# q and k of the first attention in three fp32r passes from operands that GpSimd splits

## The chip, the cores and the metric

One core of one Trainium2 chip. The time is device microseconds of one execution of the whole program. The engines are TensorE (PE; PEld is its weight load), VectorE (DVE), ScalarE (ACT), GpSimd (POOL) and SyncE (SP, which issues the DMAs).

## What is computed

Two transformer layers on x of shape (8, 512, 128), each an attention and a feed-forward part with a residual and a layernorm behind each. The change touches the projections of the first attention only:

```
qkv = x @ W_qkv                                  # (8, 512, 128) @ (128, 384), fp32
q, k, v = jnp.split(qkv, 3, axis=-1)             # 16 heads of 8
scores = einsum('bhnd,bhmd->bhnm', q, k) / sqrt(128)
out = einsum('bhnm,bhmd->bhnd', softmax(scores), v)
x = layernorm(x + out)
```

The kernel takes q and k on as exact sums of three bf16 parts, so the projections have to come out in nearly full fp32 precision.

## The kernel before

Each engine runs one program of its own, and semaphores tie them together. `attention0` (from L304) is a software pipeline over the eight batches, walked by `walk` (L282) in the same way on every engine: a step has 32 units u, and a unit takes two of the 64 turns of S1. It starts with a lead step of batch -1, which has no softmax work, and a loop of three rounds holds two steps each. While step b does S2 (`s2`, L636: scores with the row maximum folded in), the exponentials on ACT (L497) and the product with v (`pv`, L650) of batch b, it also does S1 of the batch ahead (`s1`, L572: scores for the row maximum alone, one 128x512 tile a turn) and brings in the batch after that. DVE takes the maximum of each S1 tile straight from PSUM (`reduce_max`, L735, L741), one instruction a turn.

S1 tiles and guests share three PSUM banks in turn (`FB`, `TURNS`, `BANK`). A guest stands in the list ahead of the turn that `GUEST_AT` gives: v at 16, q at 25, k at 33. `free_bank` (L582) makes PE wait until the turn that had the same bank before, three places back in the list, is taken out of it. After every two units four products with v stand between two S1 tiles on PE.

`qk_product` (L566) is one fp32 matmul of 128x512: `w[:, n, :]` is the stationary operand and `xt`, the batch's x with the model dimension on the partitions, the moving one. It waits for the load of `xt` alone. ACT copies the result to `qk` (`take_qk`, L476), and POOL splits that into three bf16 parts (`split_qk`, L819, by `split_in_parts`, L270), which SP writes to DRAM and reads back stacked by heads. Batch 0 is projected in another way ahead of the pipeline (L698).

POOL takes its work strictly in the order of its program. In a step this is (`units`, L829): the split of the row maxima (`split_max`), the residual add and layernorm of the batch behind (`add_x`, `layernorm_pool`, `layernorm_apply_pool`, L166 to L176), then `split_qk` of q and of k for batch b + 2, then the other half of the row maxima. The layernorm follows DVE's statistics, which stand in DVE's program at turn 16 (`STATS_AT`). SP loads `xt` of batch b + 2 at the start of its step b (`load_xt`, L382). Ahead of the loop, SP's `load_more` (L480) waits until all weights of the later stages are in. The same fp32r split of an x on POOL exists already at the end of this stage (`Front.gpsimd`, L957 and L960), and `hidden_lo` and the expert products use fp32r operands in three passes (L1979 to L1981).

Of the kernel before, what the change touches and what calls it, by code (L numbers as in the profile page):

```python
# [303 lines left out]
def attention0(outer, nc, g, x_t, w_qkv, select, load_more, more_in, e, m, wide):  # L304
# [4 lines left out]
    with ExitStack() as ctx:  # L309
# [3 lines left out]
        def sem(name):  # L313
            return outer.enter_context(nc.semaphore("a0_" + name))
# [15 lines left out]
        sel = prob[:, PSLOTS - 1, :, :].rearrange("p i t -> p (i t)").bitcast(BF16)[:, 0:2 * PARTS * PLACED * (HALF + QKR)]  # L330
        sel = sel.rearrange("p (n a j m) -> p n a j m", n=2, a=PARTS, j=PLACED)
        pool_gate = sb("pool_gate", [P, 1])
        nmax = sb("nmax", [P, 2, 2, HH * NT // 2])
        mrest = sb("mrest", [P, 2, HH * NT // 2])
        msplit = sb("msplit", [P, 2, PARTS, HH * NT // 2], BF16)
# [6 lines left out]

        w_in, x_in, xt_in = sem("w_in"), g["x_in"], [sem(f"xt_in{i}") for i in range(2)]
        cleared = sem("cleared")
        q_done, k_done, v_done = sem("q_done"), sem("k_done"), sem("v_done")
        q_taken, k_taken, v_taken = sem("q_taken"), sem("k_taken"), sem("v_taken")
        split, parts_done = sem("split"), sem("parts_done")
# [191 lines left out]
        def _(pe):  # L539
# [25 lines left out]

            def qk_product(b, p, n):  # L566

                pe.wait_ge(xt_in[p], 8 * (b - p) + 16)
                nc.tensor.matmul(ps_f[:, BANK["qk"[n]], :], w[:, n, :], xt[p][:, :], start=True,
                                 stop=True).then_inc((q_done, k_done)[n], 1)  # L570

            def s1(b, p, n, bank):  # L572

# [217 lines left out]
        @block.gpsimd  # L791
        def _(pool):
            pool.sem_inc(parts_done, 2 + PARTS_C)
            pool.sem_inc(parts_out, 2 * OUT_C)
            pool.sem_inc(split, 6)
            pool.sem_inc(mt_parts, MP_C)

            def split_max(b, half_no):

                k = 2 * b + half_no  # L800
                src = nmax[:, half_no, :, :]
                zero = g["zero"][:, :].unsqueeze(2).broadcast_to(list(mrest.shape))
                pool.wait_ge(mt_done, k)
                pool.wait_ge(max_done, S1_N * b + S1_N // 2 * (half_no + 1))
                nc.gpsimd.tensor_tensor(msplit[:, :, 0, :], src, zero, ALU.add).then_inc(mt_chain, 1)  # L805
                pool.wait_ge(mt_chain, 3 * k + 1)
                nc.gpsimd.tensor_tensor(mrest[:, :, :], src, msplit[:, :, 0, :], ALU.subtract).then_inc(mt_chain, 1)
                pool.wait_ge(mt_chain, 3 * k + 2)
                nc.gpsimd.tensor_tensor(msplit[:, :, 1, :], mrest[:, :, :], zero, ALU.add).then_inc(mt_chain, 1)
                pool.wait_ge(mt_chain, 3 * k + 3)  # L810
                nc.gpsimd.tensor_tensor(msplit[:, :, 2, :], mrest[:, :, :], msplit[:, :, 1, :],
                                        ALU.subtract).then_inc(mt_parts, 1)

            def add_x(b):

                pool.wait_ge(att_done, NO * (b + 1) + ATT_C)
                nc.gpsimd.tensor_tensor(att[:, :, :], att[:, :, :], X[:, b, :, :], ALU.add).then_inc(sum_done, 1)

            def split_qk(b, n):  # L819

                if isinstance(b, int) and b == 1:
                    pool.wait_ge(first_out[0], OUT_C // 2)
                    pool.wait_ge(first_out[1], OUT_C // 2)
                pool.wait_ge(parts_out, OUT_C * b + OUT_C)
                pool.wait_ge((q_taken, k_taken)[n], b + 1)
                split_in_parts(pool, nc.gpsimd, qk[:, n, :], rest[:, n, :], parts[:, n, :, :], 2 * b + n, split,
                               parts_done, g["zero"][:, :].broadcast_to([P, T]))

            def units(b, p, u0, u1, qk_on, fore, back, tail):  # L829
                if u0 == 0 and back:  # L830
                    split_max(b, 1)
                if u0 == 0 and is_first(b):
                    front.split_weight(pool, 0)
                if u0 == 0 and tail:
                    add_x(b - 1)
                    layernorm_pool(nc, pool, g, ln, b - 1)
                    layernorm_apply_pool(nc, pool, g, ln, b - 1, att, pool_gate)
                if u1 == NU and qk_on:
                    split_qk(b + 2, 0)
                    split_qk(b + 2, 1)  # L840
                if u1 == NU and fore:
                    if isinstance(b, int) and b == NB - 2:
                        pool.wait_ge(ln["x_done"], NB - 1)
                        front.split_weight(pool, 1)
                        front.split_weight(pool, 2)
                    split_max(b + 1, 0)
                    if isinstance(b, int) and b == NB - 2:
                        front.split_weight(pool, 3)
                        front.split_weight(pool, 4)
                        front.split_weight(pool, 5)  # L850
                if u1 == NU and is_last(b):
                    front.gpsimd(pool)

            pool.wait_ge(x_in, 16)
            walk(pool, units)

# [1721 lines left out]
```

## Time and profile before

| | |
|---|---|
| median of 3 runs (lowest to highest) | 1043.27 us (1043.18 to 1043.75) |
| span of the profiled execution | 1041.4 us |
| own time of the profiled execution | not listed apart from its span; the median stands 1.87 us above the span |
| busy: PE, DVE, ACT, POOL | 96%, 80%, 70%, 46% of the span |
| first attention | about 0 to 400 us of the span |
| one step of its loop | 44.15 us |

The busy share of an engine is its share of the span over all four stages. PE's busy time is modelled and counts the drain of each matmul, so two matmuls that follow each other overlap in it. What a turn costs is read from the starts of instructions instead, and from the idle time in front of them, which the timeline gives in brackets with the engine that ended it. A matmul of fp32 operands is recorded as two matmuls (x2), one of fp32r or bf16 operands as one.

### The profile page before, as it was taken

The numbers are of one execution on the slowest core, as the hardware profiler recorded it, in microseconds if no ns is written. First come the engines' busy times: TensorE is split into PE (matmuls) and PEld (weight loads), VectorE is DVE, ScalarE is ACT, GpSimd is POOL, SyncE is SP. The second block draws the span as 40 slices with busy tenths as digits, with TensorE's granted clock in tenths as the row PEclk, the third lists the DMA queues.
The fourth block names the chain that finished last, engine by engine and source line by source line (L and its number), as shares of the span: only waits on it lengthen the run. The fifth ranks groups of instructions, "written<-read, shape, count | busy, mean of one in ns | idle before, by whom it ended". The sixth has DMA issues, their size and how long they took to land. (4 is left out here: it accounts for less than half of the span.)

```text
span 1041.4 us, 20120 instructions
## 1 busy us (share of the span) xinstructions
PE 995.5 (96%) x5835; PEld 475.4 (46%) x5835; DVE 834.0 (80%) x1874; ACT 729.9 (70%) x939; POOL 475.6 (46%) x483
## 2 busy tenths in 40 slices
PE   8899999999999999999999999999999999999996
PEld 3222222222222235888888887873332333222485
DVE  6889999999999977787888789897666666643677
ACT  2078777787777786555555555568898888899754
POOL 0332514325053725676777677576442244220275
PEclk9999999999999999999999999999999999999998
DMA  6553222131321003344324323443512331230011
GB/s 198 153 186 119 76 76 89 44 117 46 96 78 52 3 2 101 102 128 145 101 91 156 121 90 117 137 137 102 172 65 61 121 119 63 60 122 1 1 31 52
DMA packets 73981, 97.04 MB, mean 93 GB/s; under 512 B 12669, under 2 KB 42237, under 8 KB 73533
## 3 DMA queue, kind: packets, MB, share of 16 engines
q1 hardware_dynamic: 73928, 96.40, 29.7%
q8 instruction: 26, 0.43, 0.2%
q14 instruction: 27, 0.21, 0.1%
HBM read 68.18 MB, written 27.79 MB: 92 GB/s over the span
## 5 line engine op out<-in xcount | busy, mean ns | idle before, releaser
L741 DVE TENSOR_REDUCE a_nmax<-a_ps_f 128x1 f32<-128x512 f32 x512 | 320.1, 683 | 20.2 <-PE a_ps_f L579 19.7
L497 ACT ACTIVATE a_prob<-a_ps_s 128x1024 f32<-128x1024 f32 x256 | 251.7, 1023 | 77.8 <-PE a_ps_s L646 76.5
L1367 ACT ACTIVATE a_prob<-a_ps_s 128x1024 f32<-128x1024 f32 x256 | 244.4, 1026 | 28.0 <-PE a_ps_s L1419 26.7
L2187 POOL TENSOR_TENSOR moe_hl<-moe_hid,moe_hh 128x512 fp32r<-128x512 f32 x134 | 173.9, 1303 | 84.3 <-ACT moe_hh L2068 84.2
L579 PE MATMUL a_ps_f<-a_ks,a_qs 48*128 48x512 bf16 x512 | 157.9, 386 | 11.8 <-DVE a_nmax L741 4.3
L2058 ACT ACTIVATE moe_ps<-moe_ps 128x512 f32<-128x512 f32 x128 | 74.5, 582 | 111.5 <-PE moe_ps L1981 110.7
L1432 PE MATMUL a_ps_o<-a_prob,a_va 128*32 128x512 f32 x1024 | 136.4, 605 | 1.4 <-DVE a_turned_o L1547 0.5
L659 PE MATMUL a_ps_o<-a_prob,a_va 128*32 128x512 f32 x1024 | 136.4, 605 | 0.5 <-ACT a_prob L497 0.4
L646 PE MATMUL a_ps_s<-a_qs,a_ks 51*128 51x512 bf16 x512 | 132.5, 381 | 1.7 <-ACT a_prob L497 1.5
L579 PEld LDWEIGHTS a_ps_f<-a_ks,a_qs 48*128 48x128 bf16 x512 | 39.7, 93 | 192.2 <-DVE a_nmax L741 162.2
L2109 DVE TENSOR_TENSOR moe_prod<-moe_cw,moe_ps 128x512 f32<-128x512 f32 x128 | 87.2, 681 | 27.4 <-PE moe_ps L1981 26.7
L1419 PE MATMUL a_ps_s<-a_qs,a_ks 48*128 48x512 bf16 x512 | 91.1, 384 | 12.0 <-ACT a_prob L1367 10.3
L2118 DVE TENSOR_TENSOR moe_hid<-moe_prod,moe_ps 128x512 f32<-128x512 f32 x128 | 86.9, 679 | 6.1 <-DVE moe_prod L2109 1.9
L2068 ACT ACTIVATE moe_hh<-moe_hid 128x512 fp32r<-128x512 f32 x136 | 84.9, 624 | 6.0 <-DVE moe_hid L2118 5.8
L277 POOL TENSOR_TENSOR a_parts<-a_qk,g_zero 128x512 bf16<-128x512 f32 x28 | 29.2, 1044 | 118.6 <-DVE a_qk L1529 60.8
L1419 PEld LDWEIGHTS a_ps_s<-a_qs,a_ks 48*128 48x128 bf16 x512 | 23.1, 93 | 130.0 <-ACT a_prob L1367 105.4
L805 POOL TENSOR_TENSOR a_msplit<-a_nmax,g_zero 128x32 bf16<-128x32 f32 x16 | 3.8, 238 | 144.9 <-DVE a_nmax L741 144.9
L1979 PE MATMUL moe_ps<-moe_xh,moe_whig 128*128 (+1 forms) x136 | 55.0, 405 | 1.3 <-DVE moe_hid L2118 1.3
L2006 PE MATMUL moe_ps<-moe_hl,moe_whid 128*128 128x512 f32 x136 | 53.9, 397 | 1.0 <-POOL moe_hl L2187 1.0
L1979 PE MATMUL moe_ps<-moe_xh,moe_whiu 128*128 (+1 forms) x136 | 53.7, 395 | 0.0
L2001 PE MATMUL moe_ps<-moe_hh,moe_wlod 128*128 128x512 f32 x136 | 53.7, 395 | 0.0
L1980 PE MATMUL moe_ps<-moe_xh,moe_wlog 128*128 (+1 forms) x136 | 53.7, 395 | 0.0
(302 smaller groups left out, 1640.1 us busy)
## 6 DMA issues: line engine op xcount, KB each, us to landing
moe_cw<-r_weights SPq DMA_DIRECT2D x256, 128.0 KB, 2.9
parts_q<-a_parts SPq DMA_DIRECT2D x48, 256.0 KB, 2.5
parts_k<-a_parts SPq DMA_DIRECT2D x48, 256.0 KB, 2.5
a_qs<-parts_q SPq DMA_DIRECT2D x126, 96.0 KB, 2.4
a_ks<-parts_k SPq DMA_DIRECT2D x126, 96.0 KB, 2.5
a_xt<-in_x_t SPq DMA_DIRECT2D x8, 256.0 KB, 2.8
out_x<-g_X SPq DMA_DIRECT2D x7, 256.0 KB, 2.3
moe_wg<-in_wg SPq DMA_DIRECT2D x1, 1088.0 KB, 6.6
```

The source lines that it names most:

```text
L497: nc.scalar.activation(prob[:, u % PSLOTS, :, :], ps_s[:, u % 2, :, :], ACT.Exp, scale=float(P) ** -0.5).then_inc(exp_done, 1)
L579: nc.tensor.matmul(ps_f[:, bank, :], stack_rows(qs[p], h, QKR)[:, qt * P:(qt + 1) * P], stack_rows(ks[p], h, QKR), start=True, stop=True). ...
L646: mm = nc.tensor.matmul(ps_s[:, u % 2, i, :], stack_rows(ks[p], h, MXR)[:, kt * P:(kt + 1) * P], stack_rows(qs[p], h, MXR), start=True, st ...
L659: mm = nc.tensor.matmul(ps_o[j * CT:(j + 1) * CT, :], v_of_head(va[p], kt, grp * HG + j), prob[:, (2 * e + j // UN) % PSLOTS, j % UN, :], ...
L741: nc.vector.tensor_reduce(nmax[:, half_no, h % 2, col:col + 1], ps_f[:, bank, :], AX.X, ALU.max, negate=True).then_inc(max_done, 1)
L1367: nc.scalar.activation(prob[:, u % PSLOTS, :, :], ps_s[:, u % 2, :, :], ACT.Sigmoid, scale=float(HD) ** -0.5).then_inc(exp_done, 1)
L1419: mm = nc.tensor.matmul(ps_s[:, u % 2, i, :], stack_rows(ks[p], h, QKR)[:, kt * P:(kt + 1) * P], stack_rows(qs[p], h, QKR), start=True, st ...
L1432: mm = nc.tensor.matmul(ps_o[j * CT:(j + 1) * CT, :], v_of_head(va[p], kt, grp * HG + j), prob[:, (2 * e + j // UN) % PSLOTS, j % UN, :], ...
L1979: nc.tensor.matmul(dst, w[0][:, j, :], hi, start=True, stop=False)
L2109: nc.vector.tensor_tensor(prod[:, bank(j), :], cw[:, slot(j), :], ps_u[:, bank(j), :], ALU.mult).then_inc(prod_done, 1)
L2118: nc.vector.tensor_tensor(hid[:, hid_at(j), :], prod[:, bank(j), :], ps_g[:, bank(j), :], ALU.mult).then_inc(hid_done, 1)
L2187: nc.gpsimd.tensor_tensor(hl[:, part_at(j), :], hid[:, hid_at(j), :], hh[:, part_at(j), :], ALU.subtract).then_inc(hl_done, 1)
```

## The change

q and k of batches 1 to 7 are computed from split operands. POOL splits the q and k columns of the weights once at the start (`part_w`: wh is w rounded to fp32r, wl the rest), and each batch's x ahead of its products (`part_x`: xh and xl, one buffer each). PE computes wh.xh + wl.xh + wh.xl in three matmuls into the same bank and waits for `x_parted`, which POOL raises, where it waited for the load. In a step, `part_x` stands in POOL's program between the layernorm of the batch behind and `split_qk`. Batch 0 and v are as before.

```diff
+        wh, wl = (sb(name, [P, 2, P], F32R) for name in ("wh", "wl"))
+        xh, xl = (sb(name, [P, T], F32R) for name in ("xh", "xl"))
...
             def qk_product(b, p, n):

-                pe.wait_ge(xt_in[p], 8 * (b - p) + 16)
-                nc.tensor.matmul(ps_f[:, BANK["qk"[n]], :], w[:, n, :], xt[p][:, :], start=True,
-                                 stop=True).then_inc((q_done, k_done)[n], 1)
+                dst = ps_f[:, BANK["qk"[n]], :]
+                pe.wait_ge(x_parted, 2 * b)
+                nc.tensor.matmul(dst, wh[:, n, :], xh[:, :], start=True, stop=False)
+                nc.tensor.matmul(dst, wl[:, n, :], xh[:, :], start=False, stop=False)
+                nc.tensor.matmul(dst, wh[:, n, :], xl[:, :], start=False, stop=True).then_inc((q_done, k_done)[n], 1)
...
+            def part_w():
+
+                src, zero = w[:, 0:2, :], g["zero"][:, :].unsqueeze(2).broadcast_to([P, 2, P])
+                pool.wait_ge(w_in, 16)
+                nc.gpsimd.tensor_tensor(wh[:, :, :], src, zero, ALU.add).then_inc(w_parted, 1)
+                pool.wait_ge(w_parted, 1)
+                nc.gpsimd.tensor_tensor(wl[:, :, :], src, wh[:, :, :], ALU.subtract).then_inc(w_parted, 1)
+                pool.wait_ge(w_parted, 2)
+
+            def part_x(b, p):
+
+                pool.wait_ge(xt_in[p], 8 * (b - p) + 16)
+                pool.wait_ge(k_done, b)
+                nc.gpsimd.tensor_tensor(xh[:, :], xt[p][:, :], g["zero"][:, :].broadcast_to([P, T]),
+                                        ALU.add).then_inc(x_parted, 1)
+                pool.wait_ge(x_parted, 2 * b - 1)
+                nc.gpsimd.tensor_tensor(xl[:, :], xt[p][:, :], xh[:, :], ALU.subtract).then_inc(x_parted, 1)
...
                 if u1 == NU and qk_on:
+                    if not (isinstance(b, int) and b < 0):
+                        part_x(b + 2, p)
                     split_qk(b + 2, 0)
                     split_qk(b + 2, 1)
...
+            part_w()
+            part_x(1, 1)
             pool.wait_ge(x_in, 16)
             walk(pool, units)
```

POOL, from the layernorm of the batch behind to the first part of q, in the loop's first round. A row has the line, the operation, out<-in and the semaphores waited for; `a_qk` is q or k in fp32, `a_parts` its bf16 parts, `g_X` the layernorm's result. Before:

```order
L171 TENSOR_TENSOR moe_y<-moe_y,a_mv 128x512 [waits a0_ln_pool]
L175 TENSOR_TENSOR a_pool_gate<-g_zero 128x1 [waits a0_ln_centred]
L176 TENSOR_TENSOR g_X<-moe_y,a_rstd 128x512
L824 ISA
L825 REGISTER_ALU [waits a0_parts_out]
L277 TENSOR_TENSOR a_parts<-a_qk,g_zero 128x512 [waits a0_q_taken]
```

With the change:

```order
L171 TENSOR_TENSOR moe_y<-moe_y,a_mv 128x512 [waits a0_ln_pool]
L175 TENSOR_TENSOR a_pool_gate<-g_zero 128x1 [waits a0_ln_centred]
L176 TENSOR_TENSOR g_X<-moe_y,a_rstd 128x512
L847 TENSOR_TENSOR a_xh<-a_xt,g_zero 128x512 [waits a0_k_done,a0_xt_in1]
L849 ISA
L850 TENSOR_TENSOR a_xl<-a_xt,a_xh 128x512 [waits a0_x_parted]
L829 ISA
L830 REGISTER_ALU [waits a0_parts_out]
L277 TENSOR_TENSOR a_parts<-a_qk,g_zero 128x512 [waits a0_q_taken]
```

Two tensor operations now stand behind the layernorm's last one, `g_X`, and ahead of the split of q, and the first of them waits for the load of `xt` and for k of the batch before.

PE at the turn of q in the loop's first step (`a_qs`, `a_ks` are the stacked parts of S1 and S2, `a_ps_f` the three shared banks, `a_ps_s` the bank of S2). Before:

```order
L579 MATMUL a_ps_f<-a_ks,a_qs 128x512 [waits a0_stack_in1]
L589 REGISTER_ALU
L568 ISA [waits a0_max_done]
L569 MATMUL a_ps_f<-a_xt,a_w 128x512 [waits a0_xt_in0]
L589 REGISTER_ALU
L579 MATMUL a_ps_f<-a_ks,a_qs 128x512 [waits a0_max_done]
L643 REGISTER_ALU
L646 MATMUL a_ps_s<-a_qs_74,a_ks_75 128x512 [waits a0_exp_done]
```

With the change:

```order
L584 MATMUL a_ps_f<-a_ks,a_qs 128x512 [waits a0_stack_in1]
L594 REGISTER_ALU
L572 REGISTER_ALU [waits a0_max_done]
L573 MATMUL a_ps_f<-a_xh,a_wh 128x512 [waits a0_x_parted]
L574 MATMUL a_ps_f<-a_xh,a_wl 128x512
L575 MATMUL a_ps_f<-a_xl,a_wh 128x512
L594 REGISTER_ALU
L584 MATMUL a_ps_f<-a_ks,a_qs 128x512 [waits a0_max_done]
```

The place in PE's order is the same; one fp32 matmul that waited for a DMA has become three that wait for POOL, with S1's next tile and S2 behind them.

## Rows read from the trace of the kernel before

**Rows 1.** The page: span, and busy time of each engine

```profile
span 1041.4 us, 20120 instructions
...
PE 995.5 (96%) x5835; PEld 475.4 (46%) x5835; DVE 834.0 (80%) x1874; ACT 729.9 (70%) x939; POOL 475.6 (46%) x483
```

**Rows 2.** Windows, one step: us, then each engine's busy time, PEclk, DMA, GB/s

```profile
111.00:155.15 44.15, 42.70 (x282) 11.62 (x278) 42.54 (x80) 34.69 (x40) 15.36 (x23) 1.00 0.27 80
```

**Rows 3.** Waits of DVE, 0 to 330 us: total us, times, longest

```profile
DVE a_nmax L741 <- PE a_ps_f L579: 18.3, 43, 2.4
```

**Rows 4.** Timeline of POOL, steps of batches 3 and 7: start, length, engine, line

```profile
113.14 1.04 POOL L176 TENSOR_TENSOR g_X<-moe_y,a_rstd 128x512 f32 x1
116.67 1.04 POOL L277 TENSOR_TENSOR a_parts<-a_qk,g_zero 128x512 bf16<-128x512 f32 x1 [2.49 <-ACT a_qk L469]
...
289.76 1.04 POOL L176 TENSOR_TENSOR g_X<-moe_y,a_rstd 128x512 f32 x1
```

**Rows 5.** Timeline of PE around q of batch 3, and q of batch 7

```profile
114.53 0.38 PE L579 MATMUL a_ps_f<-a_ks,a_qs 48*128 48x512 bf16 x1
114.83 1.13 PE L569 MATMUL a_ps_f<-a_xt,a_w 128*128 128x512 f32 x2
115.89 0.39 PE L579 MATMUL a_ps_f<-a_ks,a_qs 48*128 48x512 bf16 x1
...
116.12 0.38 PE L579 MATMUL a_ps_f<-a_ks,a_qs 48*128 48x512 bf16 x1
...
117.43 0.39 PE L579 MATMUL a_ps_f<-a_ks,a_qs 48*128 48x512 bf16 x1
...
291.45 1.12 PE L569 MATMUL a_ps_f<-a_xt,a_w 128*128 128x512 f32 x2
```

**Rows 6.** Timeline of DVE, the same turns, q to k of batch 3

```profile
110.34 5.67 DVE L741 TENSOR_REDUCE a_nmax<-a_ps_f 128x1 f32<-128x512 f32 x9
116.32 1.29 DVE L741 TENSOR_REDUCE a_nmax<-a_ps_f 128x1 f32<-128x512 f32 x2 [0.31 <-PE a_ps_f L579]
117.85 3.77 DVE L741 TENSOR_REDUCE a_nmax<-a_ps_f 128x1 f32<-128x512 f32 x6 [0.25 <-PE a_ps_f L579]
121.94 1.29 DVE L741 TENSOR_REDUCE a_nmax<-a_ps_f 128x1 f32<-128x512 f32 x2 [0.31 <-PE a_ps_f L579]
```

**Rows 7.** Instructions of L957 and L960: min/median/max ns

```profile
L957 POOL TENSOR_TENSOR moe_xh<-a_xt,g_zero x3: 1038/1038/1081, 391.2 to 397.8; 128x512 fp32r<-128x512 f32 x3
...
L960 POOL TENSOR_TENSOR moe_xl<-a_xt,moe_xh x3: 1265/1266/1272, 392.3 to 399.0; 128x512 fp32r<-128x512 f32 x3
```

**Rows 8.** Timeline of PE in the feed-forward stage: fp32r passes after a pause

```profile
503.65 0.47 PE L1979 MATMUL moe_ps<-moe_xh,moe_whig 128*128 x1
503.96 0.39 PE L1980 MATMUL moe_ps<-moe_xh,moe_wlog 128*128 x1
504.19 0.40 PE L1981 MATMUL moe_ps<-moe_xl,moe_whig 128*128 x1
```

**Rows 9.** Batch 2: SP's load, its DMA's us to landing, and PE's q

```profile
66.76 0.36 SPq L383 DMA_DIRECT2D a_xt<-in_x_t  x1
...
a_xt<-in_x_t SPq DMA_DIRECT2D x1, 256.0 KB, 2.8
...
70.69 1.12 PE L569 MATMUL a_ps_f<-a_xt,a_w 128*128 128x512 f32 x2
```

**Rows 10.** Lead step: POOL, PE, and a window (columns as in rows 2)

```profile
31.25 1.04 POOL L277 TENSOR_TENSOR a_parts<-a_qk,g_zero 128x512 bf16<-128x512 f32 x1 [30.34 <-DMA g_X<-in_x]
...
41.36 0.24 POOL L811 TENSOR_TENSOR a_msplit<-a_mrest,a_msplit 128x32 bf16<-128x32 f32 x1
...
41.75 0.23 PE L557 MATMUL a_ps_f<-a_identb,a_msplit 128*96 128x128 bf16 x1 [2.57 <-POOL a_msplit L811]
...
42.30:45.90 3.60, 3.60 (x11) 0.74 (x12) 1.98 (x3) 0.05 (x1) 0.00 (x0) 0.54 0.52 169
```

**Rows 11.** Groups by line: DVE's subtractions in the start

```profile
L783 DVE TENSOR_TENSOR a_parts<-a_rest,a_parts 128x256 bf16<-128x256 f32 x4 | 1.7, 422 | 0.2 <-ACT a_parts L527 0.2
```

More of the change, by code:

```diff
@@ L344, in attention0 @@
         cleared = sem("cleared")
+        w_parted, x_parted = sem("w_parted"), sem("x_parted")
         q_done, k_done, v_done = sem("q_done"), sem("k_done"), sem("v_done")
```

## The prediction

> **What bounds the kernel now.** The page is read first [rows 1]: all four compute engines are busy for much of the 1041.4 us, PE for 96%, so the shares decide nothing, and the stage of the change has to be read by itself. One step of its loop takes 44.15 us, of which DVE is busy 42.54 [rows 2]. PE shows 42.70 of modelled busy time, in which overlaps hide small waits, so I go by DVE's idle time: it tells where the step loses time to something other than the row maxima. DVE waits 18.3 us for S1 tiles in the stage, in 43 pieces [rows 3]. The timelines show where: behind q DVE stands idle 0.31 us, and again 0.25 us two tiles later; behind k the same pair begins with 0.31 us [rows 6]. Everywhere else around them it runs tile after tile. So the step is paced by DVE, one tile in about 0.63 us (5.67 us for nine, [rows 6]), except at the guests, where PE is late by a few tenths.
>
> The rows on PE say what q costs it: q starts at 114.83 and the next S1 tile at 115.89, 1.06 us later [rows 5]. The rows on POOL say how close the engine is that the change gives work to: its last layernorm operation ends at 113.14 + 1.04 = 114.18, only 0.65 us before q starts, and it waits 2.49 us after that for ACT's copy of q [rows 4]. That POOL idles much of a step does not help, since its idle time lies behind the place where the new work must be done.
>
> **The change, part by part.** My sum goes against the profiled span of 1041.4 us; the median of the runs shown, 1043.27, is 1.87 above it, and I carry that over unchanged.
>
> *The wait for POOL, batches 3 to 7.* `part_x` stands behind the layernorm in POOL's order, and q on PE now waits for both its operations. Their kind and shape are in the trace: 1.04 us for the high part and 1.27 for the low part, and the first of each start 1.1 us apart, at 391.2 and 392.3 [rows 7]. From POOL's end to the start of a PE instruction that waits for it took 41.75 - (41.36 + 0.24) = 0.15 us [rows 10]. So q can start 1.1 + 1.27 + 0.15 = 2.52 us behind the layernorm: at 114.18 + 2.52 = 116.70 where it starts at 114.83 now, 1.87 late. The last of the five batches gives the same: 289.76 + 1.04 + 2.52 = 293.32 against 291.45 [rows 4, 5]. Nothing moves the layernorm earlier: it hangs on DVE's statistics at turn 16, nine tiles ahead of q.
>
> *The product.* Three fp32r passes after a pause of PE started 503.65, 503.96, 504.19: 0.31 for the first, then 0.23 each [rows 8]. That makes 0.31 + 0.23 + 0.23 = 0.77 us to the next instruction, against 1.06: 0.29 less for each of 14 products. The ends are 0.69 (no extra on the first pass) and 1.06 (no gain).
>
> *q, together.* The next S1 tile comes 1.87 - 0.29 = 1.58 us later than before. Behind PE's wait stand that tile, S2 of the next unit and the products with v, so ACT and DVE both run dry: DVE has nothing left at 110.34 + 5.67 = 116.01 and was fed again at 116.32 [rows 6]. All the 1.58 us is added to DVE's idle time, and DVE works without a pause behind it, so nothing recovers it: 5 x 1.58 = 7.9 us.
>
> *q of batch 2.* No layernorm stands ahead of it, but its load comes late: issued at 66.76 and 2.8 us to landing, so at 69.56; q follows at 70.69 [rows 9]. With 2.52 us between them q starts at 72.08, 1.39 late, less 0.29: 1.1 us.
>
> *k of batches 2 to 7.* xh and xl are ready long before k. It would be easy to take 0.29 us for each, but the second S1 tile behind k needs the bank that DVE leaves with the last of the six tiles, at 117.85 + 3.77 = 121.62 [rows 6], and starts as soon as that allows. The four products with v stand behind that tile, and the tile after them therefore comes no earlier: DVE's first wait shrinks and its second grows. The same pattern is shown at q: tiles at 115.89, 116.12, and the third only at 117.43 [rows 5]. I take 0; the other end is the full 0.29, in all 6 x 0.29 = 1.7 us less.
>
> *Batch 1.* Its two products lie in the lead step, which ends in a wait of PE for POOL until 41.75 [rows 10]. POOL's chain to that point starts when the load of X lands, at 31.25 [rows 10], and `part_w` and `part_x(1, 1)` run before it, in time in which POOL waited 30.34 us. So 0 both for the gain on PE and for the added work.
>
> *The start.* While POOL splits w and the first x, DVE makes the last parts of batch 0, four operations on two SBUF inputs of 0.42 us each [rows 11]. No row has these beside POOL's work. Below, they overlap without effect; above, the two that are followed by nothing else of their half double, 0.8 us. I take 0, since the lead step's end waits for DMA and POOL anyway. The Trainium skill (GPSIMD Engine Reference, section Specifications) says that GpSimd's SBUF interfaces are shared with VectorE and contend with VectorE instructions that have two SBUF inputs. By that rule the sum would get up to the 0.8 us; in the loop it changes nothing, as DVE's row maxima there read PSUM.
>
> Everything behind q on POOL and SP (parts, stacks, row maxima) moves with q and k and keeps its room. The sum is 7.9 + 1.1 = **9.0 us**: a span of 1050.4 us, and 1043.27 + 9.0 = **1052.3 us**.
>
> **The rivals.**
>
> *The pause also costs PE its clock.* PE's new pause at q lasts some 2 us (from 114.53 + 0.38 to 116.70). The one longer pause in the stage, 2.57 us ahead of 41.75, was followed by 3.60 us at a mean granted clock of 0.54, so mostly at 1.2 instead of 2.4 GHz [rows 10], whereas the small waits of a step leave it at 1.00 [rows 2]. The new pause is nearer to the former. Lost would be (1 - 0.54) x 3.6 = 1.66 us for each pause where PE is as nearly bound as here: with all six 9.0 + 10.0 = 19.0, that is 1062.3 us; with two or three of them 1055 to 1058. The Trainium skill (TensorE: Matmul & The Clock Gate, section HAM oscillation) tells of this as a pattern: pauses between bursts of matmuls throw the clock back to the lower level, each time anew. By that rule it would be the higher sums; the lead step's pause agrees with it, and no row shows a pause of 2 us. Against it: PE is dense on both sides of q.
>
> *Part of it is made up.* If PE gains on DVE after the pause, and the waits that DVE still has in a step go (44.15 - 42.54 = 1.6 us in all, some 1.1 of them behind q), a batch loses only 0.5 us: 5 x 0.5 + 1.1 = 3.6, or 1046.9 us. Against it: PE and DVE restart from the same point as now, only later.
>
> *The splits are hidden, and it is not slower.* If PE reached q 1.87 us or more later than the layernorm's end allows now, say because DVE's statistics or POOL's spans are earlier than the records put them, q would not wait, and 13 or 14 shorter products would give between 0 and 14 x 0.29 = 4.1 us: 1039.2 to 1043.3. It is decided by the room between layernorm and q: 2.52 us is needed, and 0.65 is there in each of the five steps [rows 4, 5]. Only the roughness of POOL's spans speaks for it.
>
> **How the numbers follow.** Forecast 0.72, clock 0.13, made up 0.09, hidden 0.03, and 0.03 for a cost I don't see. The forecast's own bounds are k's 1.7 us below, six first passes of 0.08 less, and the start's 0.8 above; with them and the clock falling in up to four of six pauses the range is 1049 to 1060 us, which leaves out the case that the time is made up, the hidden one, and the worst clock. About 0.2% (2.1 us) is what a measurement of this kernel can tell from no change. The forecast, the clock and the made-up case all lie above that: slower 0.95. The hidden case is split: faster 0.02, same 0.03.
>
> **What would show it.** Right: in each loop step POOL's two new operations directly behind L176, 1.04 and 1.27 us; PE idle about 1.9 us at L573 with POOL named as the releaser, six times; three passes with 0.77 us to the next S1; DVE's wait behind q near 1.9 us instead of 0.31; steps of about 45.7 us instead of 44.15. Behind k, the sum of DVE's two waits unchanged at 0.56. Wrong: no wait at L573, or a granted clock near 0.5 behind it, a step that stays at 44.15, or DVE's other waits gone.

## The result, and the profile after

The changed kernel takes 1056.35 us (median of 5 runs, 1053.6 to 1060.0) against 1043.57 before (5 runs, 1043.2 to 1043.8): a ratio of 1.0122, 95% interval 1.0107 to 1.0137, so 12.8 us or 1.2% slower. Forecast were 1052.3 us and a range of 1049 to 1060. One run among the experiments below (of "all of it", 1102.6 us at a granted clock of 0.849) was in a slower state and is left out of every comparison. The page of the changed kernel, span and busy times [rows 1]:

```profile
span 1053.7 us, 20171 instructions
...
PE 1000.4 (95%) x5849; PEld 477.6 (45%) x5849; DVE 835.4 (79%) x1874; ACT 729.6 (69%) x939; POOL 493.0 (47%) x499
```

The span is 12.3 us longer, though PE has only 5 us more of (modelled) work and DVE 1.4. The growth is idle time. The waits of PE in the first 345 us (total us, times, longest), and those of DVE [rows 3, where the window is 330 us, as the stage ends 12 us sooner]:

```profile
PE a_ps_f L573 <- POOL a_xl L850: 8.4, 5, 1.7
```

```profile
DVE a_nmax L746 <- PE a_ps_f L584: 27.4, 38, 2.3
```

PE has a wait for POOL's `a_xl` that did not exist, five times and up to 1.7 us, and DVE's waits for S1 tiles have gone from 18.3 to 27.4 us. The timelines show one of the five, q of batch 3: POOL, then PE, then DVE [rows 4, 5, 6].

```profile
114.79 1.04 POOL L176 TENSOR_TENSOR g_X<-moe_y,a_rstd 128x512 f32 x1
115.78 1.04 POOL L847 TENSOR_TENSOR a_xh<-a_xt,g_zero 128x512 fp32r<-128x512 f32 x1
116.90 1.26 POOL L850 TENSOR_TENSOR a_xl<-a_xt,a_xh 128x512 fp32r<-128x512 f32 x1
```

```profile
116.17 0.38 PE L584 MATMUL a_ps_f<-a_ks,a_qs 48*128 48x512 bf16 x1
118.22 0.50 PE L573 MATMUL a_ps_f<-a_xh,a_wh 128*128 128x512 f32 x1 [1.67 <-POOL a_xl L850]
118.55 0.39 PE L574 MATMUL a_ps_f<-a_xh,a_wl 128*128 128x512 f32 x1
118.78 0.40 PE L575 MATMUL a_ps_f<-a_xl,a_wh 128*128 128x512 f32 x1
119.11 0.39 PE L584 MATMUL a_ps_f<-a_ks,a_qs 48*128 48x512 bf16 x1
```

```profile
111.98 5.66 DVE L746 TENSOR_REDUCE a_nmax<-a_ps_f 128x1 f32<-128x512 f32 x9
119.53 1.29 DVE L746 TENSOR_REDUCE a_nmax<-a_ps_f 128x1 f32<-128x512 f32 x2 [1.88 <-PE a_ps_f L584]
121.07 3.78 DVE L746 TENSOR_REDUCE a_nmax<-a_ps_f 128x1 f32<-128x512 f32 x6 [0.25 <-PE a_ps_f L584]
125.00 1.29 DVE L746 TENSOR_REDUCE a_nmax<-a_ps_f 128x1 f32<-128x512 f32 x2 [0.16 <-PE a_ps_f L584]
126.64 1.89 DVE L746 TENSOR_REDUCE a_nmax<-a_ps_f 128x1 f32<-128x512 f32 x3 [0.35 <-PE a_ps_f L584]
```

POOL does its two new operations directly behind the layernorm, which ends at 114.79 + 1.04 = 115.83. q starts at 118.22, 2.39 us behind it, where it was 0.65 us behind; the next S1 tile comes 0.89 us after q's first pass, where it was 1.06. DVE's wait behind q is 1.88 us instead of 0.31. Behind k the first of its two waits is 0.16 instead of 0.31 and the second, at 126.64, is 0.35.

The same row of PE for q of batches 2, 4, 5, 6 and 7:

```profile
72.44 0.49 PE L573 MATMUL a_ps_f<-a_xh,a_wh 128*128 128x512 f32 x1
...
163.91 0.50 PE L573 MATMUL a_ps_f<-a_xh,a_wh 128*128 128x512 f32 x1 [1.68 <-POOL a_xl L850]
...
209.59 0.50 PE L573 MATMUL a_ps_f<-a_xh,a_wh 128*128 128x512 f32 x1 [1.67 <-POOL a_xl L850]
...
256.79 0.50 PE L573 MATMUL a_ps_f<-a_xh,a_wh 128*128 128x512 f32 x1 [1.67 <-POOL a_xl L850]
...
303.71 0.50 PE L573 MATMUL a_ps_f<-a_xh,a_wh 128*128 128x512 f32 x1 [1.67 <-POOL a_xl L850]
```

From q to q the steps (with 118.22 for batch 3) are 45.78, 45.69, 45.68, 47.20 and 46.92 us; before, they were 44.14 to 44.17. So there is a constant 1.54 us, and 1.51 and 1.23 us more in two steps. The windows tell these two apart (busy times of PE, PEld, DVE, ACT and POOL, then granted clock, DMA share, GB/s): in the first units of batch 0, and behind q of batches 3, 5 and 6.

```profile
56.60:63.40 6.80, 6.45 (x27) 0.95 (x29) 3.92 (x7) 2.94 (x4) 3.33 (x5) 0.50 0.85 332
118.40:121.80 3.40, 3.29 (x22) 0.95 (x21) 2.02 (x4) 2.00 (x3) 1.83 (x2) 1.00 0.00 0
210.20:213.60 3.40, 3.40 (x16) 0.46 (x16) 1.29 (x2) 1.62 (x2) 2.10 (x2) 0.50 0.00 0
258.00:261.40 3.40, 3.40 (x18) 0.63 (x15) 1.80 (x3) 1.42 (x3) 2.78 (x3) 0.50 0.00 0
```

Behind q of batch 3 PE goes on at full clock; behind q of batches 5 and 6 it works for some 3.4 us at a granted clock of 0.50, the 1.2 GHz level. Below, such a stretch is called a fall. Another one, 6.8 us long, lies in the first units of batch 0 (56.6 to 63.4 us).

The sum of the profile, by the starts of the products that make v: the one of batch 2 starts at 66.23 instead of 64.48 us (+1.75), the step from it to the next one, with q of batch 2 in it, is 0.1 us shorter, five steps are longer by 1.54 (+7.7), two of them by a further 1.51 and 1.24 (+2.75), and behind the last there are 712.2 us left against 712.0. That makes 12.3 us.

### The profile page after: what moved, and what is told of

It reads as the page before. It is cut to its first block and busy times, and to the rows that moved or that the text cites. A ratio compares the mean times of both kernels' runs of the same rounds, so it can differ in the third digit from the quotient of the medians.

```text
span 1053.7 us, 20171 instructions
## 1 busy us (share of the span) xinstructions
PE 1000.4 (95%) x5849; PEld 477.6 (45%) x5849; DVE 835.4 (79%) x1874; ACT 729.6 (69%) x939; POOL 493.0 (47%) x499
## 5 line engine op out<-in xcount | busy, mean ns | idle before, releaser
L584 PE MATMUL a_ps_f<-a_ks,a_qs 48*128 48x512 bf16 x512 | 160.1, 389 | 12.0 <-DVE a_nmax L746 4.1
L664 PE MATMUL a_ps_o<-a_prob,a_va 128*32 128x512 f32 x1024 | 139.8, 619 | 0.5 <-ACT a_prob L500 0.4
L1459 PE MATMUL a_ps_o<-a_prob,a_va 128*32 128x512 f32 x1024 | 136.4, 605 | 1.4 <-DVE a_turned_o L1574 0.5
L2136 DVE TENSOR_TENSOR moe_prod<-moe_cw,moe_ps 128x512 f32<-128x512 f32 x128 | 87.2, 681 | 27.4 <-PE moe_ps L2008 26.7
```

The source lines that it names most:

```text
L584: nc.tensor.matmul(ps_f[:, bank, :], stack_rows(qs[p], h, QKR)[:, qt * P:(qt + 1) * P], stack_rows(ks[p], h, QKR), start=True, stop=True). ...
L664: mm = nc.tensor.matmul(ps_o[j * CT:(j + 1) * CT, :], v_of_head(va[p], kt, grp * HG + j), prob[:, (2 * e + j // UN) % PSLOTS, j % UN, :], ...
L1459: mm = nc.tensor.matmul(ps_o[j * CT:(j + 1) * CT, :], v_of_head(va[p], kt, grp * HG + j), prob[:, (2 * e + j // UN) % PSLOTS, j % UN, :], ...
L2136: nc.vector.tensor_tensor(prod[:, bank(j), :], cw[:, slot(j), :], ps_u[:, bank(j), :], ALU.mult).then_inc(prod_done, 1)
```

## The experiments

The theory from the profile was this: the five steps lose 1.54 us each to POOL's order; which pauses also cost PE its clock is chance; the passes themselves give nearly nothing; the start delays nothing but may shift the clock. The rivals were that the splits cost wherever they stand, that the passes give their full 0.17 to 0.29 us, and that the falls of the clock have nothing to do with the pauses. Edits below are against the changed kernel, where nothing else is said, and are cut at "...".

The table holds the starts of one v product to the next, as the traces have them, for the steps that bring in batches 2 to 7 (us), and the median times. "Before" had medians of 1043.5 to 1044.1 beside them, on chips where its own runs ranged from 1040.8 to 1048.1. A ratio is an estimate from all runs of both kernels and not the quotient of their medians; the two can differ by 0.2%.

| kernel | steps | time, ratio to before (95%) |
|---|---|---|
| before | 44.17 44.15 44.16 44.15 44.16 44.15 | |
| changed | 44.06 45.68 45.69 47.20 46.93 45.69 | 1056.35, 1.0122 (1.0107 to 1.0137) |
| changed, again | 44.07 45.69 47.27 47.07 46.81 45.71 | 1056.72, 1.0099 (1.0074 to 1.0124) |
| start's splits alone | 44.18 44.16 44.17 44.17 44.18 44.16 | 1041.20, 0.9973 (0.9957 to 0.9989) |
| passes alone | 44.07 44.08 44.06 44.06 44.08 44.06 | 1043.48, 1.0000 (0.9983 to 1.0018) |
| wait alone | 46.41 47.50 47.52 47.30 47.14 45.91 | 1058.19 (one run) |
| pause filled | 45.46 45.69 45.71 45.69 45.69 45.70 | 1050.74, 1.0071 (1.0048 to 1.0095) |
| start later | 44.07 46.82 45.70 46.84 45.69 47.08 | 1055.38, 1.0110 (1.0080 to 1.0140) |
| two waits | 45.41 45.25 45.25 45.25 45.24 45.25 | 1048.37, 1.0039 (1.0020 to 1.0058) |
| split ahead of the layernorm | 44.06 44.06 44.06 44.06 44.05 44.06 | 1044.14, 0.9997 (0.9985 to 1.0009) |
| lead step filled (on before) | 44.17 44.16 44.16 44.16 44.16 44.16 | 1042.30, 0.9979 (0.9967 to 0.9992) |
| all of it | 48.78 44.07 44.06 44.07 44.07 44.07 | 1045.52, 1.0004 (0.9993 to 1.0016) |
| all, start as changed, load sooner | 44.20 44.07 44.07 44.07 44.07 44.07 | 1041.84, 0.9975 (0.9963 to 0.9988) |
| the same, denser first units | 44.05 44.06 44.06 44.06 44.06 44.06 | 1042.32, 0.9980 (0.9969 to 0.9991) |

**The start's splits alone.**

```diff
 qk_product: one fp32 matmul, as before
...
-                    if not (isinstance(b, int) and b < 0):
-                        part_x(b + 2, p)
```

> The kernel before with only the splits at the start (w's two operations and the first x's two), the products in fp32 as before; nothing reads the split operands. Theory A (the start's contention is hidden): DVE's pair of subtractions at the start takes 2.2 us instead of 0.8, PE idles there and falls to half clock, S1 starts 3 us late, and all of it goes into the lead step's wait for POOL, so the time is 1043.6 within 1.5 us. Theory B (the start costs): the step of batch 0 begins in another place of the clock's rhythm, the clock falls around 56 to 63 us, and the time is 1045 to 1047 us. If the pair of subtractions stays at 0.8 us, POOL is not what slowed it.

Neither: its median is 2.3 us below before. DVE's first two subtractions of parts with POOL's low part of x, and PE's lead step (its wait for POOL, and the first S2 of batch 0):

```profile
7.75 0.41 DVE L786 TENSOR_TENSOR a_parts<-a_rest,a_parts 128x256 bf16<-128x256 f32 x1
8.31 1.25 DVE L786 TENSOR_TENSOR a_parts<-a_rest,a_parts 128x256 bf16<-128x256 f32 x1
...
7.75 1.54 POOL L848 TENSOR_TENSOR a_xl<-a_xt,a_xh 128x512 fp32r<-128x512 f32 x1
```

```profile
40.55 0.23 PE L560 MATMUL a_ps_f<-a_identb,a_msplit 128*96 128x128 bf16 x1 [0.63 <-POOL a_msplit L814]
...
51.20 0.39 PE L649 MATMUL a_ps_s<-a_qs,a_ks 51*128 51x512 bf16 x2
```

Both subtractions stand beside POOL's low part of x (7.75 to 9.29); the second took 1.25 us, the first 0.41. S1 starts 0.73 us later by that (13.35 against 12.62), and in this profile POOL is ready 1.2 us sooner as well, since X landed at 30.05 and not at 31.25. So the pause in the lead step is 0.63 us instead of 2.57 [rows 10]. No fall of the clock follows at 42 us, and batch 0 starts at 51.20 instead of 53.70; 1.2 of these 2.5 us are X's landing. The delay I feared is absorbed, and spares a pause besides. The gain stands in the median alone: the profiled run took 1043.0 us, for it has a fall at 55.0 to 61.8 us that the kernel before has not in its profile.

**The lead step's wait filled**, on the kernel before, asks whether that pause is what the 2.3 us were.

```diff
 turn_max:
+                if half_no == 0 and isinstance(b, int) and b == 0:
+                    warm_up(9)
                 pe.wait_ge(mt_parts, 2 * b + half_no + 1 + MP_C)
```

> The kernel before with nine matmuls of the identity ahead of the one wait of the lead step in which PE stands idle for 2.57 us; nothing else. It tests why the start's splits made the kernel 2.3 us faster. Theory A (by coming later to that wait PE has a short pause there, and its clock does not fall behind it): no fall at 42 to 46 us, 1040.5 to 1042 us. Theory B (something else in the start): the same as before, 1043.2 to 1043.8 us.

1042.3 against 1044.1, 0.3 us above A's interval, and the fall at 42 us is gone from the trace: theory A rather than B. A fall at 56 to 63 us stands in this profile, and the profiled run (1044.96) was no faster than before; the gain is that of the medians.

**The passes alone.** This kernel leaves out the splits of x in the loop, and computes q and k of batches 2 to 7 from batch 1's x.

```diff
-                pe.wait_ge(x_parted, 2 * b)
+                pe.wait_ge(x_parted, 2)
...
-                    if not (isinstance(b, int) and b < 0):
-                        part_x(b + 2, p)
...
+            pool.wait_ge(first_low, 4)
             part_w()
```

> The three passes without the loop's splits: x is split for batch 1 alone (and only after DVE's last parts of batch 0), and q and k of batches 2 to 7 are computed from batch 1's x. No pause at q. Theory A (the bank and the products with v behind the guest give the gain back): the steps stay at 44.1 us within 0.1, the time at 1043 to 1044 us. Theory B (every product counts): 0.17 to 0.29 us less for each of 13 products, steps 0.3 to 0.6 us shorter, 1039.8 to 1041.4 us.

Theory A: steps of 44.07 us against 44.16, so both products together give 0.09 us a step, and the time does not move. PE at q of batch 3:

```profile
118.15 0.50 PE L573 MATMUL a_ps_f<-a_xh,a_wh 128*128 128x512 f32 x1
...
119.05 0.39 PE L584 MATMUL a_ps_f<-a_ks,a_qs 48*128 48x512 bf16 x1
119.38 0.39 PE L584 MATMUL a_ps_f<-a_ks,a_qs 48*128 48x512 bf16 x1
```

and DVE over the same turns:

```profile
113.66 7.10 DVE L746 TENSOR_REDUCE a_nmax<-a_ps_f 128x1 f32<-128x512 f32 x11
121.12 5.21 DVE L746 TENSOR_REDUCE a_nmax<-a_ps_f 128x1 f32<-128x512 f32 x8 [0.37 <-PE a_ps_f L584]
```

The three passes take 0.90 us to the next tile, 0.16 less than the fp32 matmul, but the tile after that comes 0.33 us behind it instead of 0.23 [rows 5]. I take this to be the wait for its bank, which the trace does not name: DVE's eleven tiles at 0.64 us each put the end of the ninth, whose bank it needs, at about 119.4. The products with v stand behind it. DVE's first wait behind q is gone, and its second has grown from 0.25 to 0.37.

**The wait alone**, with the splits and fp32 products. The edit of `qk_product` is shown against the kernel before:

```diff
 qk_product:
+                pe.wait_ge(x_parted, 2 * b)
                 pe.wait_ge(xt_in[p], 8 * (b - p) + 16)
                 nc.tensor.matmul(ps_f[:, BANK["qk"[n]], :], w[:, n, :], xt[p][:, :], start=True,
```

> The changed kernel with its splits and PE's wait for them, but the products in fp32 as before. Theory A (the pause is the loss and the passes give 0.1 to 0.17 us back a step): steps without a fall at 45.8 to 45.95 us, against 45.69 with the passes and 44.16 before. If the passes did more than that, steps of 46.2 us or more.

Of the five steps of batches 3 to 7, the one without a fall takes 45.91 us, 1.75 above before, in theory A's interval; the passes give 0.22 of that back. Four of these five pauses brought a fall, which cost 1.2 to 1.6 us each. The longest pause of this kernel, at q of batch 2, brought none (the granted clock is 1.00 behind it):

```profile
70.82 1.12 PE L573 MATMUL a_ps_f<-a_xt,a_w 128*128 128x512 f32 x2 [2.20 <-POOL a_xl L849]
```

**The pause filled.**

```diff
 qk_product:
+                if n == 0 and not (isinstance(b, int) and b == 1):
+                    columns = identb[:, :].unsqueeze(1).broadcast_to([P, NT, P])
+                    for _ in range(6):
+                        nc.tensor.matmul(dst, identb[:, :], columns, start=True, stop=True)
                 pe.wait_ge(x_parted, 2 * b)
```

> The changed kernel with six matmuls of the identity into q's own bank ahead of PE's wait for POOL (batches 2 to 7), so that PE works through most of the pause; q starts no earlier. Theory A (part of the loss is PE's clock, which falls behind some of the pauses): no fall behind a q, all five later steps at 45.6 to 45.8 us, the time 1.4 us lower for each fall that is gone: 1051 to 1054 us with a smaller spread than the changed kernel's 1053.6 to 1060.0. Theory B (the falls have nothing to do with the pause): falls behind q stay, steps of 47 us stay, 1053.6 to 1060 us.

PE at q of batch 3, and the window from the next tile on:

```profile
114.27 1.47 PE L575 MATMUL a_ps_f<-a_identb 128*128 128x512 bf16 x6
116.01 0.50 PE L577 MATMUL a_ps_f<-a_xh,a_wh 128*128 128x512 f32 x1 [0.27 <-POOL a_xl L854]
...
116.90 0.39 PE L588 MATMUL a_ps_f<-a_ks,a_qs 48*128 48x512 bf16 x1
```

```profile
116.70:120.20 3.50, 3.37 (x26) 0.90 (x28) 2.63 (x5) 2.60 (x4) 2.36 (x3) 1.00 0.00 0
```

PE works through the pause and waits 0.27 us at its end. q comes no earlier, all five steps take 45.69 to 45.71 us, and no fall is left behind any q. The time is 1050.74 us, a little under A's interval and 5.6 us below the changed kernel's median. Not all of that is the clock behind q. The two profiles differ by 5.0 us. The two falls behind q are 2.7 of it. Another 3.6 us lie ahead of the v product of batch 2 (62.62 against 66.23), mostly the fall at 56.6, which this profile has not and which the added matmuls, all behind that place, cannot have removed. And 1.4 us go the other way, since PE now comes to q of batch 2 ahead of POOL (a step of 45.46 against 44.06). So it is shown that the falls behind q belong to the pause, at 1.1 to 1.6 us each; that filling it saves 5.6 us is in part a start without a fall.

**The changed kernel once more**, for where the falls are.

> The changed kernel once more, beside the others on one chip. Steps without a fall at 45.69 us again; falls behind other q than in the first profile, if it is chance which pause brings one; 1053 to 1060 us, with steps of about 46.8 to 47.2 us where a fall is.

Three steps have a fall, behind q of batches 4, 5 and 6; the first of the windows:

```profile
165.30:168.70 3.40, 3.40 (x15) 0.53 (x14) 1.29 (x2) 1.62 (x2) 1.69 (x2) 0.54 0.00 0
```

Batches 5 and 6 in the first profile, 4, 5 and 6 in this one, 3, 5 and 7 with the later start: the pause is the same each time (1.67 us in PE's waits), and it is not fixed which of them a fall follows. What decides it stays open.

**Two waits.**

```diff
-                pe.wait_ge(x_parted, 2 * b)
+                pe.wait_ge(x_parted, 2 * b - 1)
                 nc.tensor.matmul(dst, wh[:, n, :], xh[:, :], start=True, stop=False)
                 nc.tensor.matmul(dst, wl[:, n, :], xh[:, :], start=False, stop=False)
+                pe.wait_ge(x_parted, 2 * b)
                 nc.tensor.matmul(dst, wh[:, n, :], xl[:, :], start=False, stop=True).then_inc((q_done, k_done)[n], 1)
```

> The changed kernel with PE's wait parted: the two passes on xh wait for xh alone, the third for xl. xl is ready as late as now, so the third pass starts as late as xl, but the two others (0.57 us) are done by then. Theory A (pause and passes add up as in the timeline): the next S1 tile comes about 0.5 us earlier a step, steps of 45.1 to 45.3 us instead of 45.69; and the pause falls into two of some 0.6 and 0.7 us, behind which the clock does not fall: 1047 to 1050 us. Theory B (the clock falls by PE's work in the whole stretch, not by the length of one pause): steps of 45.1 to 45.3 us between falls, but falls behind some q as now, 1050 to 1056 us.

```profile
114.24 0.50 PE L573 MATMUL a_ps_f<-a_xh,a_wh 128*128 128x512 f32 x1 [0.33 <-POOL a_xh L848]
...
115.60 0.50 PE L576 MATMUL a_ps_f<-a_xl,a_wh 128*128 128x512 f32 x1 [0.62 <-POOL a_xl L851]
116.03 0.39 PE L585 MATMUL a_ps_f<-a_ks,a_qs 48*128 48x512 bf16 x1
```

Steps of 45.25 us as expected, waits of 0.33 and 0.62 us, and no fall in the profile. That is theory A, as far as one profile goes: it is of the fastest of six runs (1047.6 us, mean granted clock 0.997), and the slowest, 1050.35 us at 0.992, lies in B's interval. Falls in other runs are not ruled out.

**The start's splits later.**

```diff
+            pool.wait_ge(first_low, 4)
             part_w()
             part_x(1, 1)
```

> The changed kernel with the splits at the start held back until DVE has made the last parts of batch 0. Theory A (the start's contention costs by way of the clock): DVE's pair is back at 0.8 us, S1 starts at 12.6, no fall at 56 to 63 us, the time falls by 1 to 3 us against the changed kernel beside it. Theory B (the start is hidden): same time as the changed kernel within the spread of its runs.

1055.38 us is inside the changed kernel's spread, and its profile has a fall at 40.5 to 47.5 us in place of those at 12 and at 56.5 us. The contention is gone (DVE's pair takes 0.84 us), but S1 starts early again, PE's pause in the lead step is 2.90 us, and the fall at 40.5 us follows it. The time is not lower: B rather than A, though 1 us could not be told.

**The split ahead of the layernorm**, with POOL's loop written out so that batches 3 to 7 alone have it.

```diff
                     add_x(b - 1)
+                    if b + 2 < NB:
+                        part_x(b + 2, p)
                     layernorm_pool(nc, pool, g, ln, b - 1)
...
-                    if not (isinstance(b, int) and b < 0):
+                    if b == 0:
                         part_x(b + 2, p)
...
-            walk(pool, units)
...
```

> The changed kernel with POOL's split of x moved in each loop step from behind the layernorm to ahead of it (behind the residual add, where POOL waits 4.2 us for DVE's statistics); POOL's loop is written out for that. Theory A (the place in POOL's order is the whole loss): PE waits at q at most for batch 2, the steps are 44.07 us as with the passes alone, and the time is that of the kernel with only the start's splits less 0.1 a step: 1040.5 to 1043 us. Theory B (splitting x costs wherever it stands, by a later layernorm or by slowing DVE): steps of 45 us or more, 1047 us or more.

POOL in the step of batch 3, and PE at q:

```profile
107.70 1.04 POOL L847 TENSOR_TENSOR a_xh<-a_xt,g_zero 128x512 fp32r<-128x512 f32 x1
108.82 1.28 POOL L850 TENSOR_TENSOR a_xl<-a_xt,a_xh 128x512 fp32r<-128x512 f32 x1
112.05 0.20 POOL L183 TENSOR_TENSOR a_ve<-a_mv,g_eps 128x4 f32<-128x4 f32 x1 [1.94 <-DVE a_mv L153]
...
114.70 1.04 POOL L176 TENSOR_TENSOR g_X<-moe_y,a_rstd 128x512 f32<-128x512 f32 x1
```

```profile
116.07 0.38 PE L584 MATMUL a_ps_f<-a_ks,a_qs 48*128 48x512 bf16 x1
116.39 0.49 PE L573 MATMUL a_ps_f<-a_xh,a_wh 128*128 128x512 f32 x1
```

The two operations fit into POOL's wait for DVE's statistics, which is 1.94 us now instead of 4.20; the layernorm still ends 0.65 us ahead of q (115.74 and 116.39), and PE does not wait. Steps of 44.06 us: the place in POOL's order was the whole loss of the loop. (POOL's loop written out, by itself, was not run.) The time, 1044.14, is above A's interval. The profiled run (1044.44) has two falls of the clock in the first 65 us, at 43, behind a pause of 1.55 us in the lead step, and at 56.5.

**All of it**: this, the later start and the filled lead step.

> All of it: x split ahead of the layernorm, the start's splits held back until DVE has its last parts of batch 0, and the lead step's wait filled with nine matmuls. Theory A of all three: no pause of PE over 1 us in the stage but possibly at q of batch 2, steps of 44.07 us, 1040 to 1042 us, at or below the kernel before with the lead step's wait filled. If splitting costs by itself: 1047 us or more.

1045.5 us, and in the profile A's "but possibly" is the reason. With an earlier start PE comes to q of batch 2 before its x is loaded and split:

```profile
71.56 0.80 PE L575 MATMUL a_ps_f<-a_xh,a_wh 128*128 128x512 f32 x1 [2.53 <-POOL a_xl L852]
```

A pause of 2.53 us, then the passes at half clock and a step of 48.78. This is the term for batch 2 that the first profile did not show.

**The same with the start as changed, and SP's waits for the weights behind the loop**, so that batch 2's x is asked for sooner.

```diff
 load_more:
-                sp.wait_ge(moe_in, 2 * 16)
-                sp.wait_ge(c1_in, 8 * 16)
...
 all_in:
+                sp.wait_ge(moe_in, 2 * 16)
+                sp.wait_ge(c1_in, 8 * 16)
```

`load_more` (L2480) waits for the loads of the second attention and for two small ones of the feed-forward stage, not for all weights of the later stages; the others are waited for behind the loop already (`all_in`).

> x split ahead of the layernorm, the lead step's wait filled with nine matmuls, and SP's waits for the later stages' weights moved behind the loop, so that batch 2's x is loaded some 10 us earlier. Theory A (the pauses of PE are what is lost: at q by POOL's order, at q of batch 2 by the load, in the lead step by X): no pause at any q, steps of 44.06 us, a fall of the clock at most around 56 to 64 us; 1040 to 1043 us and below the kernel before on this chip. Theory B (the falls in the first 65 us come anyway): 1043 to 1045 us, no better than the kernel before.

PE at q of batch 2:

```profile
70.36 0.50 PE L575 MATMUL a_ps_f<-a_xh,a_wh 128*128 128x512 f32 x1 [0.18 <-POOL a_xl L852]
```

1041.84 us, 0.25% below before by the ratio, with 0.18 us of wait at q of batch 2 and no fall in the stage. The load was issued at 59.63 us and took 8.2 us to land instead of 2.8 [rows 9], I take it behind the weights, so it came some 2 us sooner and not 10. This beats both kernels, but the lead step's filled wait alone gives nearly as much (0.9979 against 0.9975, intervals that overlap).

**Denser first units.**

```diff
+                    if back and is_first(b) and u < 3:
+                        warm_up(2)
```

> The same with two matmuls of the identity more in each of the first three units of batch 0, where PE has S1 and S2 alone and no product with v yet. Theory A (the fall around 56 to 64 us comes from how thin PE's work is there): that fall is gone too, spread of the runs under 1.5 us, 1039 to 1041.5 us. Theory B: the fall stays and the time is that of the run without these matmuls or up to 1.5 us above.

B: 1042.32 us, runs from 1042.0 to 1044.6, much as without it (1041.5 to 1044.6). The profile has no fall there, with or without them. What brings the fall around 56 us in some runs stays open.

## Why the prediction was right, point by point

**The number.** The measured 1056.35 us is 4.1 above the forecast of 1052.3 and lies where the prediction put the rival of the clock (1055 to 1058 us, chance 0.13). It is inside the range because the upper end allowed for four falls. Two more terms missed, in opposite directions, in the changed kernel's profile: the step with q of batch 2 is 0.1 us shorter where 1.1 more was forecast, and the start 1.75 us longer where 0 was forecast. That they partly cancel is luck. The lower end, 1049, is a little below what its own terms give (1050.1).

**The wait, 5 x 1.87 us, and the product, 0.29 less.** The mechanism and the five places are as said, and so is the sum of the two, 1.58 us a step, for which the profile has 1.54. Both sizes were off, in opposite directions. q starts 2.39 us behind the layernorm and not 2.52, so it is 1.74 late instead of 1.87: POOL goes from one operation to the next and hands over a little faster than I had put it. The passes take 0.89 us to the next tile and not 0.77, since behind the third pass the next tile starts 0.33 us later and not 0.23, so they save 0.17.

**k at nothing.** Right, and it is the step that would have been easiest to get wrong: passes alone are worth 0.09 us a step for q and k together, though each of the products is 0.16 us shorter. The sign named for it holds as well: DVE's two waits behind k are 0.16 and 0.35 us in the changed kernel, 0.51 in sum, against 0.31 [rows 6] and 0.25 before:

```profile
123.47 1.89 DVE L741 TENSOR_REDUCE a_nmax<-a_ps_f 128x1 f32<-128x512 f32 x3 [0.25 <-PE a_ps_f L579]
```

**q of batch 2, 1.1 us.** It depends on the start, which I had not seen. In the changed kernel's profile PE comes there at 72.44, after POOL is done, and waits for nothing: the fall at 56.6 had made it late. With the pause filled, and no such fall in its profile, that step takes 45.46 us, 1.3 more than before; in "all of it" it is a pause of 2.53 us.

**The start at nothing, at most 0.8 us.** The bound was too small; that the added work itself is absorbed held. DVE and POOL at the start of the changed kernel (L788 is the L783 of rows 11):

```profile
7.85 0.42 DVE L784 TENSOR_TENSOR a_rest<-a_ps_s,a_parts 128x256 f32<-128x256 f32 x1 [0.43 <-ACT a_parts L526]
8.19 2.25 DVE L788 TENSOR_TENSOR a_parts<-a_rest,a_parts 128x256 bf16<-128x256 f32 x2
...
7.71 1.04 POOL L847 TENSOR_TENSOR a_xh<-a_xt,g_zero 128x512 fp32r<-128x512 f32 x1 [0.95 <-POOL a_wl L840]
8.83 1.33 POOL L850 TENSOR_TENSOR a_xl<-a_xt,a_xh 128x512 fp32r<-128x512 f32 x1
```

The two subtractions beside POOL's splits take 2.25 us instead of 0.84 [rows 11]; PE pauses for them and does the next matmuls at half clock. In PE's rows below, twelve matmuls take 4.76 us where they took 3.07; the lead step still ends at 42.35, with 0.21 us of wait, against 41.75 [rows 10]. What I missed is the clock in the first 65 us. A shorter pause in the lead step is worth something: the start's splits by themselves took 2.3 us off the median. And the fall at 56.6 us costs more than that: the v product of batch 2 starts at 66.23 us in the changed kernel, and at 62.2 to 62.6 in three profiles with the same start and no such fall (the pause filled, the wait alone, two waits).

```profile
11.21 4.76 PE L718 MATMUL a_ps_s<-a_parts,a_prob 128*112 128x512 bf16 x12 [1.74 <-DVE a_rest L784]
...
42.35 0.26 PE L560 MATMUL a_ps_f<-a_identb,a_msplit 128*96 128x128 bf16 x1 [0.21 <-DVE a_nmax L746]
```

**The rival of the clock, 0.13.** This is what the forecast lacks. It came at two or three of the five pauses, at 1.1 to 1.6 us each, where I had 1.66. With the pauses filled the kernel takes 1050.7 us; in its profile that is 9.0 us more than before (five steps at 1.54 and 1.3 for batch 2), less 1.9 for the earlier start. The 5.6 us from there to 1056.35 are the clock in two places, in the first profile 2.75 us behind q and 3.6 in the first units of batch 0, of which 1.4 come back at q of batch 2. Only the first place is the rival as I had put it. The changed kernel's runs spread over 6.4 us; that the same two causes make the spread is likely but not shown. The one pause of 2.57 us with a fall behind it stood in my rows; the right use of it was to put some falls into the likeliest case. The Trainium skill (TensorE: Matmul & The Clock Gate, section HAM oscillation) describes falls behind longer pauses, which come back each time; here only some pauses brought one.

**Made up, 0.09, and hidden, 0.03.** Neither: a step without a fall loses 1.54 us and not 0.5, so nothing is caught up, and PE waited at each of the five.

## What to carry to other kernels

Place added work in the engine's own order before pricing it by idle shares: POOL was idle more than half of the time, yet the two operations stood at the one place in its order that PE would wait for, and the same two a few lines earlier cost nothing. A shorter matmul gains only what the next instructions can use, so follow it to the second tile behind it. Where a change makes PE pause, put the clock into the likeliest case, and part or fill a pause that cannot be removed (parted in two it cost 45.25 us a step, filled 45.69, and neither profile has a fall behind a q).

## What the runs showed that I had not expected

- VectorE's subtraction of two SBUF operands took up to 1.25 us beside GpSimd's tensor operations (a pair of them 2.25), against 0.42 without them; not every one did, as one at 7.75 us in "the start's splits alone" took 0.41 beside the same operation. With POOL's splits held back the pair took 0.84. Meanwhile its subtraction of one PSUM and one SBUF operand stayed at 0.42 beside them (the one at 7.85 above, with POOL's high part of x running from 7.71). In this it agrees with the Trainium skill (GPSIMD Engine Reference, section Specifications), which names instructions with two SBUF inputs and gives no price.
- A pause of PE of 1.7 us brought the clock to the 1.2 GHz level behind some q and not behind others, in the same program and between runs of it; two waits of 0.33 and 0.62 us brought none in the one profile there is. Nor does the length of a pause alone decide it here: one of 1.55 us in the lead step brought a fall (the split ahead of the layernorm), one of 2.20 us at q of batch 2 (the wait alone) and one of 2.88 us at the start (the load sooner) brought none.
- The kernel before pays for such a fall as well: nine matmuls whose result is not used, in its lead step, make its median 1.8 us (0.2%) lower.
